# The mix of the embedding rows as side-by-side products of 64 rows, the upper layers between gram and projection, row numbers added on VectorE, late weights loaded later

## What is computed

```python
e = stack([tbl_f[ids[:, f]] for f in range(26)], axis=1)        # 2048 x 26 x 64
x = layer_norm(r_dense_t @ Wd.T, gd, bd)                        # 2048 x 128
y = layer_norm(einsum('bnd,ed->bne', e, Ws), gs, bs)
y = layer_norm(einsum('bne,pn->bep', y, Wsi), gsi, bsi)         # mix to 32
T = concatenate([x[:, None, :], swapaxes(y, 1, 2)], axis=1)     # 33 vectors
Z = einsum('bnd,bmd->bnm', T, T)[:, TRIL_I, TRIL_J]             # 528 products
z = layer_norm(Z @ Wl.T, gl, bl)[:, :384]
h = relu(concatenate([z, r_dense_t], axis=1) @ W_top1 + b_top1)
y = relu(h @ W_top2 + b_top2) @ W_top3
```

## Time and profile before

| | |
|---|---|
| three runs | 572.38, 572.98 and 573.72 us, median 572.98 |
| profiled execution | span 572.2 us from the first to the last instruction |
| PE busy | 509.5 us (89%) |
| DVE, POOL, ACT busy | 400.8 us (70%), 400.9 us (70%), 280.8 us (49%) |
| granted TensorE clock | mean 0.967 of full speed |

### The profile page before, as it was taken

One profiled execution on the slowest core, in us unless ns is written; L12 is line 12 of the kernel. 1 busy time (PEld: TensorE's weight loads), 2 busy tenths in 40 slices (PEclk: granted clock), 3 DMA queues, 4 the chain that ended last, 5 costly groups with the idle time before them and its releaser, 6 DMA issues.

```text
span 572.2 us, 17022 instructions
## 1 busy us (share of the span) xinstructions
PE 509.5 (89%) x6783; PEld 396.8 (69%) x6783; DVE 400.8 (70%) x707; ACT 280.8 (49%) x727; POOL 400.9 (70%) x423
## 2 busy tenths in 40 slices
PE   1768759899999999999999999999999999898887
PEld 1644438677868677777778687778677777777665
DVE  3747666786778878677878786878878776777720
ACT  0514553454636555455545454646455455545433
POOL 5777777777777777777777777777777777777000
PEclk9958886999999999999999999999999999999999
DMA  7711113131212213131313131222213131313020
GB/s 266 281 28 29 25 29 90 27 91 28 82 38 67 51 33 87 27 93 28 91 28 93 27 91 29 78 41 67 54 39 80 27 90 29 91 27 91 5 65 1
DMA packets 28704, 36.39 MB, mean 64 GB/s; under 512 B 10731, under 2 KB 19379, under 8 KB 28113
## 3 DMA queue, kind: packets, MB, share of 16 engines
q0 software_dynamic: 13408, 13.81, 12.6%
q1 hardware_dynamic: 15218, 21.50, 11.0%
HBM read 26.09 MB, written 9.18 MB: 62 GB/s over the span
## 4 chain that ended last, share of the span: by engine, by line
PE 22%; POOL 22%; DVE 22%; issue 19%; ACT 9%; DMA 4%; SPq 1%; DVEq 0%; ACTq 0%
POOL rows L530 22%; PE bank_z L661 7%; DVE y_var L409 5%; PE bank_d L689 4%; DVE y L399 4%; DVE r_vec L425 4%; PE bank_z L644 4%; ACT y_sq L813 3%; DVE bank_z L417 2%; ACT y_std L819 2%; DMA wsi_b<-in_wsi_b 2%; DVE scaled L364 2%; PE bank_b L631 2%; PE bank_z L604 1%; ACT h L893 1%
## 5 line engine op out<-in xcount | busy, mean ns | idle before, releaser
L530 POOL DMA_INDIRECT rows<-in_table,ids_all x416 | 398.4, 958 | 126.8 <-issue 125.9
L409 DVE TENSOR_REDUCE y_var<-y_sq 128x32 f32<-128x1024 f32 x64 | 78.1, 1220 | 45.3 <-ACT y_sq L813 45.3
L813 ACT ACTIVATE y_sq<-y 128x512 f32<-128x512 f32 x128 | 80.3, 631 | 36.7 <-DVE y L399 36.4
L631 PE MATMUL bank_b<-mixed,gs_row 64*128 64x512 f32 x128 | 74.4, 662 | 19.8 <-ACT mixed L842 19.6
L644 PEld LDWEIGHTS bank_z<-r_vec 128*32 128x32 f32 x4096 | 47.8, 111 | 59.8 <-issue 58.0
L621 PE MATMUL bank_a<-wsi_b,scaled 128*128 128x192 f32 (+3 forms) x512 | 84.0, 309 | 2.1 <-DVE scaled L389 2.0
L425 DVE TENSOR_TENSOR r_vec<-y,bank_z 128x512 f32<-128x512 f32 x128 | 82.3, 684 | 2.2
L621 PEld LDWEIGHTS bank_a<-wsi_b,scaled 128*128 128x128 f32 x512 | 78.2, 195 | 3.2 <-DVE scaled L389 3.2
L661 PE MATMUL bank_z<-wl,zd 128*128 128x512 f32 x160 | 74.7, 614 | 1.2 <-DMA zd<-zx 1.2
L835 ACT ACTIVATE row_std<-row_var,eps 128x8 f32<-128x8 f32 (+1 forms) x64 | 19.2, 300 | 113.6 <-DVE row_var L373 89.3
L631 PE MATMUL bank_c<-mixed,gs_row 64*128 64x512 f32 x128 | 74.4, 662 | 0.0
(11 more groups left out here) (111 smaller groups left out, 609.4 us busy)
## 6 DMA issues: line engine op xcount, KB each, us to landing
zx<-zs SPq DMA_DIRECT2D x15, 560.0 KB, 3.8
rows<-in_table,ids_all POOLq DMA_INDIRECT x416
dense_t<-in_dense_t SPq DMA_DIRECT2D x1, 2048.0 KB, 8.5
wl<-in_wl SPq DMA_DIRECT2D x1, 1280.0 KB
w<-in_w SPq DMA_DIRECT2D x1, 1280.0 KB, 16.3
wsi_b<-in_wsi_b SPq DMA_DIRECT2D x1, 1248.0 KB, 11.5
zd<-zx SPq DMA_DIRECT2D x15, 80.0 KB
zd<-zx SPq DMA_DIRECT2D x15, 70.0 KB
```

What stands on the lines that cost most here:

```text
L409: v.tensor_reduce(y_var[:, k % BANKS, :], y_sq[:, k % 2, :, :].rearrange("e a (s p) -> e (a s) p", p=PROJ), AX_X, ALU.add).then_inc(y_var_ ...
L530: nc.gpsimd.indirect_dma_start(rows[t % 2][:, c, D * blk:D * (blk + 1)], None, io["table"], bass.IndirectOffsetOnAxis(ap=ids_all[:, n:n + ...
L631: pe.matmul(bank_y[blk][:], gs_row[half, :], mixed[half, k % 2, :], start=True, stop=True)\
L813: nc.scalar.activation(y_sq[:, k % 2, blk, :], y[:, k % 2, blk, :], ACT.Square).then_inc(y_squared, 1)
```

## The change

Five things change together.

1. **Mix.** The 128 rows of a chunk no longer hold consecutive (sample, feature) rows but two half chunks of 64 rows, rows 0 to 63 for one 8-sample half of a bank and rows 64 to 127 for the other. Each window product becomes two products of 64 rows, one for each half, into two different PSUM banks (`bank_aw`). A quarter has 4 windows as before, now of 352 columns together instead of 608 or 640, and 8 products instead of 4. `wsi_b` has 44 window columns of 32 numbers instead of 78.
2. **Order.** `upper(w)` stands between `gram_product(w+1)` and `project(w)`; `turn_z` stays at the end of its step. In the last two quarters `first_dense(14)` goes from step 62 to step 63, ahead of `linear(14)`. On ACT `keep_out` goes to the head of its step.
3. **Banks.** `first_layer`, `second_layer` and the output share bank_d, so `first_dense(t)` waits for `out_kept` instead of `h1_kept`.
4. **Row numbers.** The row base of each table is added to the ids on DVE, first for tile 0, then for the others, instead of on POOL; ids and bases come by one transfer.
5. **Late weights.** `wl` is loaded only after `x_row0` is ready, `w1`, `w2`, `w3` after the end of preparation.

```diff
@@ chunk_windows
-        first, last = c * P // N_SP, (c * P + P - 1) // N_SP
+        first, last = c * HALF // N_SP, (c * HALF + HALF - 1) // N_SP
         while first <= last:
-            bank = first // SPB
-            end = min(last + 1, (bank + 1) * SPB)
-            n = max(end - first, 3)
...
+            bank = first // SPH
+            end = min(last + 1, (bank + 1) * SPH)
+            out.append((c, first, end - first, bank, at))
@@ banks
+        bank_aw = ctx.enter_context(nc.psum_tensor("bank_aw", [P, 2, BANK], F32))
+        bank_a = bank_aw[:, 0, :]
+        bank_w = bank_aw[:, 1, :]
+        bank_m2 = bank_aw[:, :, BANK // 2:]
-        bank_h2 = [bank_w] * (TILES - 1) + [bank_b]
+        bank_h2 = [bank_d] * (TILES - 1) + [bank_b]
@@ vector
+            dve.wait_ge(s_ids, 16)
+            add_row_base(0, 1)
+            add_row_base(1, TILES)
@@ sync
-            for dst, src in ((ids_all, "ids"), (row_base, "row_base")):
-                sp.dma_start(dst[:], io[src]).then_inc(s_ids, 16)
+            sp.dma_start(ids_based[:], io["ids_based"]).then_inc(s_ids, 16)
...
-            for dst, src in ((wl, "wl"), (mask_a, "mask_a"), (mask_b, "mask_b")):
-                sp.dma_start(dst[:], io[src]).then_inc(s_wl, 16)
+            for dst, src in ((mask_a, "mask_a"), (mask_b, "mask_b")):
+                sp.dma_start(dst[:], io[src]).then_inc(s_masks, 16)
+            sp.wait_ge(prep, prep_at["x_row0"])
+            sp.dma_start(wl[:], io["wl"]).then_inc(s_wl, 16)
+            sp.wait_ge(prep, prep_at["end"])
             for dst, src in ((w1, "w1"), (w2, "w2"), (w3, "w3")):
@@ gpsimd
-            pool.wait_ge(s_ids, 32)
-            nc.gpsimd.tensor_tensor(ids_all[:].rearrange("p (t n) -> p t n", t=TILES),
...
             def gather(k):
                 t, q = divmod(k, BANKS)
+                if k == 0:
+                    pool.wait_ge(ids_ready, 1)
+                if k == 1:
+                    pool.wait_ge(ids_ready, 2)
@@ mix
-                    o = (s0 - q * SPB) * PROJ
-                    mm = pe.matmul(bank_m[:, o:o + num * PROJ], scaled[:, c, :], wsi_b[:, w0:w0 + num, :],
-                                   start=(n == 0), stop=(n == len(wins) - 1), skip_group_check=True)
+                    o = (s0 - q * SPH) * PROJ
+                    for h in range(2):
+                        half = slice(HALF * h, HALF * (h + 1))
+                        mm = pe.matmul(bank_m2[:, h, o:o + num * PROJ], scaled[half, c, :], wsi_b[half, w0:w0 + num, :],
+                                       start=(n == 0), stop=(n == len(wins) - 1), skip_group_check=True)
@@ first_dense
                 elif t < TILES - 1:
-                    pe.wait_ge(h1_kept, t)
+                    pe.wait_ge(out_kept, t)
@@ upper
                     if 1 <= tile < TILES - 1:
                         linear(tile - 1, range(STEPS))
-                    elif tile == TILES - 1:
-                        first_dense(tile - 1)
                 if q == 3 and tile >= 1:
-                    if tile < TILES - 1:
-                        first_dense(tile - 1)
-                        turn_z(tile - 1)
-                    else:
+                    first_dense(tile - 1)
+                    if tile == TILES - 1:
                         linear(tile - 1, range(STEPS))
@@ main loop, tensor
                 if ahead:
                     gram_product(w + 1)
+                upper(w)
                 if new:
                     project(w)
...
-                upper(w)
+                if w % BANKS == 3 and 1 <= w // BANKS < TILES - 1:
+                    turn_z(w // BANKS - 1)
```

More of the change, by code:

```diff
@@ L41 @@
 MIX_BANKS = BLK // SPB
+HALF = P // 2
+SPH = SPB // 2
 QUAD = 4
@@ L72, in chunk_windows @@
     for c in range(CHUNKS):
-        first, last = c * P // N_SP, (c * P + P - 1) // N_SP
+        first, last = c * HALF // N_SP, (c * HALF + HALF - 1) // N_SP
         while first <= last:
-            bank = first // SPB
-            end = min(last + 1, (bank + 1) * SPB)
-            n = max(end - first, 3)
-            start = min(first, (bank + 1) * SPB - n)
-            out.append((c, start, n, bank, at))
-            at += n
+            bank = first // SPH
+            end = min(last + 1, (bank + 1) * SPH)
+            out.append((c, first, end - first, bank, at))
+            at += end - first
             first = end
@@ L260, in _, with add_row_base @@
             v = nc.vector
+            def add_row_base(first, end):
+                v.tensor_tensor(ids_all[:, 2 * CHUNKS * first:2 * CHUNKS * end].rearrange("p (t n) -> p t n", t=end - first),
+                                ids_all[:, 2 * CHUNKS * first:2 * CHUNKS * end].rearrange("p (t n) -> p t n", t=end - first),
+                                row_base.rearrange("p (o n) -> p o n", o=1).broadcast_to([P, end - first, 2 * CHUNKS]),
+                                ALU.add).then_inc(ids_ready, 1)
+            dve.wait_ge(s_ids, 16)
+            add_row_base(0, 1)
+            add_row_base(1, TILES)
             step(v.memset(eps[:], EPS))
@@ L315, in finish_x @@
                 dve.wait_ge(pe_prep, 8 + j)
[L316 removed]
+                step(v.tensor_scalar(x_t[:, j * BANK:(j + 1) * BANK], bank_x[j % 2], col["gd"], col["bd"],
                                      ALU.mult, ALU.add), "end" if j == 3 else f"x{j}")
@@ L347, in top_weights @@
                 dve.wait_ge(bl_done, 1)
-                step(v.tensor_tensor(b1[:], bank_w[:, 0:4], col["b1"], ALU.add))
+                step(v.tensor_tensor(b1[:], bank_d[:, 0:4], col["b1"], ALU.add))
                 for c in range(3):
@@ L584, in add_up_x @@
                     pe.wait_ge(sum_x_kept, j)
-                pe.matmul(bank_w, ones[:], x_t[:, j * BANK:(j + 1) * BANK], start=True, stop=True)\
+                pe.matmul(bank_d[:], ones[:], x_t[:, j * BANK:(j + 1) * BANK], start=True, stop=True)\
                     .then_inc(sum_x_done, 1)
@@ L697, in second_layer @@
                     pe.wait_ge(y_kept, 2 * QUARTERS)
-                elif t:
-                    pe.wait_ge(out_kept, t)
                 for k in range(2):
@@ L790, in keep_sum_x @@
                 act.wait_ge(sum_x_done, j + 1)
-                nc.scalar.copy(sum_x[SUM_X_ROW:SUM_X_ROW + 1, j * BANK:(j + 1) * BANK], bank_w[SUM_X_ROW:SUM_X_ROW + 1, :])\
+                nc.scalar.copy(sum_x[SUM_X_ROW:SUM_X_ROW + 1, j * BANK:(j + 1) * BANK], bank_d[SUM_X_ROW:SUM_X_ROW + 1, :])\
                     .then_inc(sum_x_kept, 1)
@@ L841, in keep_mixed @@
                     act.wait_ge(y_done, 2 * (k - 1))
-                nc.scalar.copy(mixed[:, k % 2, :], bank_m[:]).then_inc(mix_kept, 1)
+                nc.scalar.copy(mixed[:, k % 2, :].rearrange("p (h n) -> p h n", h=2), bank_m2).then_inc(mix_kept, 1)
             def keep_z(k):
@@ L920, in _ @@
                     relu_2(tile - 2)
+                if q == 3 and tile >= 2:
+                    keep_out(tile - 2)
                 if ahead:
@@ L936, in _ @@
                     scale_z(tile - 1)
-                if q == 3 and tile >= 2:
-                    keep_out(tile - 2)
                 if 1 <= tile < TILES and q == 1:
@@ L985, in laid_out @@
     for c, s0, k, bank, w0 in WINDOWS:
-        for r in range(P):
-            s, n = divmod(c * P + r, N_SP)
-            if s0 <= s < s0 + k and s // SPB == bank:
-                wsi_b[r, w0 + s - s0] = wsi[:, n]
+        for r in range(HALF):
+            s, n = divmod(c * HALF + r, N_SP)
+            if s0 <= s < s0 + k:
+                wsi_b[r, w0 + s - s0] = wsi_b[HALF + r, w0 + s - s0] = wsi[:, n]
     lin = np.asarray(x["L0_rec_Wl"])
```

49 lines of the change are left out of this document (24 added, 25 removed).

## The result

The changed kernel takes **646.29 us** (median of 4 runs, 644.82 to 654.3) against 573.35 us for the kernel before, run beside it (4 runs, 572.38 to 574.01): ratio 1.1297, 95% interval 1.1246 to 1.1347. The forecast was 620 us, range 594 to 655. The profiled execution has a span of 643.2 us and took 644.98.

A forecast was written before the change was run, and what follows sets the result against it. The prediction took PE to lag the gathers, which bound the end before; the new order lengthens the loop. First linear at 98.7, 13 tiles at 34.1 to 542.0, then 77.7: 619.7, plus 0.8 gives 620 us, range 594 to 655.

The forecast's parts named there:

- the start: Up to the first linear: 98.7 instead of 104.88, by 3.0 us from preparation and 3.2 from the order.
- the loop without falls: From one project's end to the next, through DVE and ACT: 34.1 us a tile instead of 30.7.
- the tail: From the linear of tile 13 to the end: 77.7 us, where it was 68.5.
- the step from the span to the median: Added at the end of the sum: the median lies 0.8 us above the profiled span.
- the likeliest case: Whole kernel: 600 to 640 us, chance 0.65, with ACT's pieces perhaps half hidden.
- a rival apart: Granted clock falls in PE's gaps, at q = 1 ahead of the gram: 642 to 664 us, chance 0.15.
- Its upper price: At q = 1, a clock fall from 2.4 to 1.2 GHz adds 1.5 to 3.0 us; this is the 3.0.
- The argument against it: Late slices stay at clock 9 despite waits like 0.87 us ahead of the last turn.
- a term that the forecast had at nothing: The shorter mix, some 1.0 us for 1.3 per quarter: in the loop this gives nothing.
- Step 62: In the tail, third layer alone, bound by DVE's round of 6.0 + 1.1: 7.1 us.
- step 63: Last project waits behind ACT's output copy, first_dense(14) and linear(14): 10.4 us.
- the rival of the serial halves: Loads of the mix's halves go one behind another: 1.6 us more in some 15 tiles, 644 us, chance 0.10.

The follow-up runs named there:

- Experiment 2: The kernel before with only the order changed, old mix and old loads kept: 626.17 us, ratio 1.0893.
- 3: The changed kernel with ACT's copy of the turned rows ahead of its pieces for the upper layers: 602.37 us, ratio 1.0501.
- 6: The changed kernel with all products of the mix issued twice: 632.71 us, ratio 1.1027.
- 9: The changed kernel with the mix issued twice only in the steps with q = 1, 16 of 64: 628.77 us, ratio 1.0953.
- 10: The changed kernel with the gram products issued twice in all steps, behind the wait: 682.22 us, ratio 1.1931.
- experiment 1: The changed kernel with the upper layers back behind interact, first_dense(14) in step 63 behind project(63): 575.82 us, ratio 1.0041.
- experiment 5: The changed kernel with the upper layers back behind interact and first_dense(14) between mix(63) and project(63): 572.61 us, ratio 0.9973.
- experiment 7: The changed kernel with only linear(14) put back behind interact(62): 641.25 us, ratio 1.1149.
- Experiment 8: The kernel before with only the row numbers on DVE and the late weight loads: 572.45 us, ratio 0.9974.
- experiment 4: The changed kernel with ACT's copy of the turned rows one step earlier, between the two squares of y: 606.84 us, ratio 1.0565.

## Why the forecast came out as it did

The forecast, 620.5 us ahead of rounding, is 25.8 us short. By the terms of its own sum: the start -3.4, the loop without falls +3.9 (13 x 34.4 against 13 x 34.1), falls of the clock in these tiles +19.7, the tail +3.3, and the step from the span to the median +2.3 (3.1 for 0.8). On the last: time and span of one execution lie 1.8 us apart in every run on record (644.98 and 643.2), so the profiled execution of the kernel before, with a span of 572.2, took 574.0 and was the slowest of its four, and 0.8 was too little. That the time fell into the range is owed to its upper end, which was set for the rivals; the likeliest case, 600 to 640 us, did not come.

**The loop was right, step by step.** In the tile from 159 to 194 us of the changed kernel, at the full clock, the first `project` row of the steps q = 1, 2, 3, 0, 1 starts at 159.32, 170.10, 177.45, 185.75 and 193.72. The steps are 10.8 (forecast 10.5), 7.4 (7.5), 8.3 (8.2) and 8.0 us (7.9): 34.4 where 34.1 was forecast. Experiment 2 shows that the order alone makes it, and 3 that ACT's pieces ahead of the copy are part of it. "Busy" had said nothing of this: PE was busy for 89% before, and the added idle time is a chain through DVE and ACT that the old order had covered.

**The term that was mis-sized is the clock.** The forecast had it as a rival apart (0.15, 642 to 664 us) and left it out of the sum. It came on top of the loop of the likeliest case: 13 tiles took 466.9 us, and 13 x 34.4 is 447.2, so **19.7 us** are falls of the clock. Of these, seven slow `second_layer` steps make about 15 us and four falls at `third_layer` and `linear` about 5. The forecast named the step with q = 1, behind the wait ahead of the gram, and not the one with q = 2. Its upper price, 3.0 us a tile, is near that of a full fall (3.2), but over all tiles the falls cost 1.5 us a tile, its lower price. The argument against it, that slices late in the kernel stay at 9 with waits of 0.87 us, was about shorter waits than the 1.5 us that the forecast itself names at q = 1 (1.55 to 1.94 in the trace). The Trainium skill (TensorE: Matmul & The Clock Gate, Part 1, on oscillation) tells of waits between groups of products after which the next group runs at half rate, in every round of a loop, and advises to keep the work together or to pad it. Its case has longer waits, for transfers; in the loops here falls follow waits of 1.03 to 1.94 us, and not in every round. Experiments 6 and 9 agree with the advice, by 13.6 and 17.5 us.

**What sets off a fall stays partly open.** Shown: in the changed kernel it hits the q = 1 step in 8 of 14 tiles and the q = 2 step in 4. At q = 1 it goes away or becomes rare when the wait there is shortened with work (6 and 9: one slow `second_layer` in 28) or by an earlier copy (3: none), when the mix is the longer one of before (2: one in 14, with waits of 1.3 to 1.7 us), and for eight tiles in a row when there is more work behind an unchanged wait of 1.84 us (10). In the changed kernel waits of 1.55 us are followed in some tiles by 1.95 us for `second_layer` and in others by 2.77. No single one of these quantities separates all cases.

**The start** is 3.4 us sooner than forecast: the first `linear` at 95.3 against 98.7. The first turn gained what was said (30.49 us, against 33.33 in the trace of before: 2.8 of the 3.0). Of the gain beyond that and the 3.2 of the order, about 3.5 us, the cause stays open. Experiment 2 (old mix) has the first `linear` at 101.5, 3.4 sooner than before, as forecast for the order (3.2), and experiment 1 (old order) at 98.5, 6.4 sooner, which would leave 3.4 us for the mix, a term that the forecast had at nothing. But experiment 5, whose kernel is that of experiment 1 up to the last steps, has it at 101.7: one execution differs from the next by 3.2 us there. The granted clock between 33 and 98 us was 0.79 in experiment 1, 0.72 in 5, 0.80 in the changed kernel and 0.75 in the one before, so part or all of it can be the clock of the start-up; that is not shown.

**The tail** from the `linear` of 13 (562.21) to the end is 81.0 us for 77.7, again by falls of the clock more than by the chain: 1.2 us at this `linear` (5.78 us), 1.5 in step 61 (9.4 for 7.9, `second_layer` 2.78) and 1.0 behind the last interact (`first_dense(15)` 3.79 us). Step 62 took 1.0 us less than forecast (6.1 for 7.1), step 63 0.8 more. Its timeline in the changed kernel:

```profile
603.62 0.24 ACT L922 COPY out_row<-bank_d 1x128 f32<-1x128 f32 x1
603.91 2.05 PE L697 MATMUL bank_d<-dense_t,w 128*128 128x128 f32 x16 [0.27 <-ACT out_row L922]
605.80 4.57 PE L678 MATMUL bank_z<-wl,zd 128*128 128x512 f32 x10
...
610.84 0.59 PE L648 MATMUL bank_c<-mixed,gs_row 64*128 64x512 f32 x1
```

`project(63)` ends 11.2 us after `project(62)` (600.24) for the 10.4 of the sum: ACT's copy ends 3.6 us after it and not 2.9. The last `project` does wait behind `first_dense(14)` and `linear(14)`, which are not needed there; with `linear(14)` moved back in experiment 7 step 63 is 5.2 us shorter (6.0 for 11.2), and the rest of the 7.4 us by which that tail is shorter are fewer falls.

**The mix in halves** runs in pairs: 16 loads in 0.97 us. By the median load of 0.188 us they would take 3.0 us one behind another, and the rival of the serial halves had them at 2.34, so it is out. The Trainium skill (TensorEngine Tiling (Array Packing), Key Properties) lets different tiles load and multiply in parallel, which this agrees with; of the drain that it puts at a change of mode no run here gives a price, and the sum closes without one.

**The gathers** were not the bound in the changed kernel (POOL waits for scaled rows), and are again in experiment 1, where the loads of `turn` wait for rows in 13 places; that is why a shorter mix and an earlier start are worth 0.3% and no more. Experiment 8 has the same 0.3% without the shorter mix.

## What to carry to other kernels

Before moving work between two products of a loop, follow the chain that starts at the second one through the other engines: work that stands beside that chain is free, and the same work ahead of its start is paid in full. Copies that release PE belong ahead of pieces that nobody waits for on the same engine, but each place has a next victim (experiment 4). Where PE gets a new wait in every round (1.55 to 1.94 us here, in a few places 1.04), count falls of the clock into the sum and not only among the rivals, and look at the products behind each wait in all tiles, not at the mean clock: a fall comes in some rounds and not in others. Before a few us are given to a cause, look whether two executions of the same stretch agree to within them.

## What the runs showed of the hardware that was not expected

Less work can be slower: with the order of the change, the kernel with the shorter mix, the new banks and the new loads is 20 us slower than the one with the old ones (646.29 against 626.17), and issuing the short mix twice in 16 steps won 17.5 us of that back. The mean granted clock shows it as 0.931 against 0.959, which looks like little; the single product group behind the wait shows it as 3.62 against 1.95 us.
